# Attention stage of a fused block: softmax sums of two branches added up by POOL, shared product sets, single exact-pass buffers

## The reference, cut to what matters

```python
o1 = _attn(q, k1, v1, causal[None, None])          # causal, 1024 keys
o2 = _attn(q, ks, vs)                              # selected, KEEP = 256 keys
o3 = _attn(q, kw, vw, winmask[None, None])         # window of 64 keys
o = g[:, 0] * o1 + g[:, 1] * o2 + g[:, 2] * o3
return o.transpose(0, 2, 1, 3).reshape(B, T, N_HEAD * VDIM) @ Wproj
```

## Time and profile before

| | |
|---|---|
| median of 3 runs | 2780.97 us (2780.05 to 2782.86) |
| the profiled execution | 2781.34 us |
| its span | 2779.4 us |
| mean granted TensorE clock | 0.908 |
| busy over the span: TensorE, its weight loads | 83%, 56% |
| busy: VectorE, ScalarE, POOL | 59%, 46%, 24% |
| DMA | 360.53 MB, mean 130 GB/s |
| exponentials, L1370 | x1600, 637.8 us in total |
| products with ones, L1344 | x3200, 512.0 us |
| products with causal values, L1344 | x1536, 284.3 us |
| reciprocals, L1425 | x192, 331.9 us |

### The profile page before, as it was taken

One profiled execution on the slowest core, in us unless ns is written; L12 is line 12 of the kernel. 1 busy time (PEld: TensorE's weight loads), 2 busy tenths in 40 slices (PEclk: granted clock), 3 DMA queues, 4 the chain that ended last, 5 costly groups with the idle time before them and its releaser, 6 DMA issues. The chain is left out here.

```text
span 2779.4 us, 45396 instructions
## 1 busy us (share of the span) xinstructions
PE 2320.6 (83%) x16656; PEld 1545.5 (56%) x16656; DVE 1628.3 (59%) x3043; ACT 1266.2 (46%) x2777; POOL 669.8 (24%) x687
## 2 busy tenths in 40 slices
PE   5585858663999999999999999999999999601995
PEld 3464545442666666666666666566566666401884
DVE  4758575734466466466566576566565564450766
ACT  2354545440455555555455455555555555310442
POOL 0265656573011011011011011011010010145332
PEclk9697978765999999999999999999999999655997
DMA  2255555479547646556655565664664660611113
GB/s 97 97 219 184 216 187 201 172 269 226 126 93 146 132 101 139 122 118 131 127 121 122 120 136 114 136 129 104 137 137 96 138 130 10 158 39 47 48 53 110
DMA packets 222841, 360.53 MB, mean 130 GB/s; under 512 B 68794, under 2 KB 124701, under 8 KB 222240
## 3 DMA queue, kind: packets, MB, share of 16 engines
q1 hardware_dynamic: 216288, 348.43, 50.1%
q0 software_dynamic: 4320, 8.43, 0.9%
q10 hardware_dynamic: 2016, 0.77, 0.2%
HBM read 229.58 MB, written 126.56 MB: 128 GB/s over the span
## 5 line engine op out<-in xcount | busy, mean ns | idle before, releaser
L1370 ACT ACTIVATE prob<-ps 128x512 f32<-128x512 f32 (+5 forms) x1600 | 637.8, 441 | 665.8 <-PE ps L1325 656.3
L1434 DVE TENSOR_REDUCE maxima<-ps 128x1 f32<-128x512 f32 (+3 forms) x768 | 387.5, 547 | 291.4 <-PE ps L1250 147.0
L1344 PE MATMUL ps<-prob,plain 128*32 128x512 f32 (+5 forms) x3200 | 512.0, 443 | 0.0
L1400 POOL TENSOR_TENSOR products<-products,sums 128x256 f32<-128x256 f32 x192 | 140.8, 733 | 1540.3 <-DVE sums L1425 1539.0
L1439 DVE TENSOR_REDUCE maxima<-ps 128x2 f32<-128x512 f32 (+1 forms) x512 | 293.7, 606 | 192.6 <-PE ps L1261 98.4
L1425 DVE RECIPROCAL sums<-sums 128x256 f32<-128x256 f32 x192 | 331.9, 1736 | 97.6 <-ACT sums L1383 97.6
L1317 PE MATMUL ps<-q1a_s,k1a_s 128*128 128x512 f32 (+3 forms) x768 | 303.0, 395 | 0.0
L1325 PE MATMUL ps<-q1b_s,k1b_s 128*128 128x512 f32 (+3 forms) x768 | 301.1, 393 | 0.0
L1344 PE MATMUL ps<-prob,v_s 128*32 128x512 f32 (+3 forms) x1536 | 284.3, 491 | 0.0
L1250 PE MATMUL ps<-k1a_s,q1a_s 128*128 128x512 f32 (+3 forms) x768 | 234.5, 374 | 0.5 <-DVE maxima L1439 0.2
L1381 ACT ACTIVATE products<-ps,gates_a 64x512 f32<-64x512 f32 x192 | 131.0, 682 | 196.4 <-PE ps L1344 196.3
(11 more groups left out here) (333 smaller groups left out, 4889.8 us busy)
## 6 DMA issues: line engine op xcount, KB each, us to landing
qh_dram<-pairs SPq DMA_DIRECT2D x96, 512.0 KB, 2.7
kwh_dram<-pairs SPq DMA_DIRECT2D x64, 512.0 KB, 2.7
qa_s<-qh_dram SPq DMA_DIRECT2D x128, 256.0 KB, 4.7
kwa_s<-kwh_dram SPq DMA_DIRECT2D x128, 256.0 KB, 7.7
q1a_s<-qh_dram SPq DMA_DIRECT2D x128, 256.0 KB, 4.8
qb_s<-qh_dram SPq DMA_DIRECT2D x64, 256.0 KB, 9.3
kwb_s<-kwh_dram SPq DMA_DIRECT2D x64, 256.0 KB, 10.3
k1a_s<-k1ah_dram SPq DMA_DIRECT2D x32, 512.0 KB, 6.9
```

The source lines that it names most:

```text
L1344: mm = pe.matmul(ps[at:at + VD, SCORES + k % 2, q0 - c * CH:q0 - c * CH + w], w_, m.prob[:, n % PROBS, h, 0:w], start=first, stop=True, sk ...
L1370: act.activation(m.prob[:, u % PROBS, h, 0:w], ps[:, turn % SCORES, 0:w], ACT.Exp, scale=SCALE).then_inc(s["exp_done"], 1)
L1400: pool.tensor_tensor(o, o, m.sums[:, br, cc], ALU.mult).then_inc(s["divided"], 1)
L1434: ins = dve.tensor_reduce(partial[:, h, i, part:part + 1], bank[:, 0:w], AX, ALU.max)
```

## The change

- SUMS is ordered window, selected, causal, and UNITS is made of groups: the window units in sets of up to two as before, each still with its own ones; then each of the eight units of selected 0, selected 1 and causal 0 is zipped with one of the eight of causal 1, of equal width.
- In a zipped group no ones are multiplied. The first unit's two heads take the lower 64 rows of a bank, the second's the upper 64: `product(side, u, NW * place, values)`.
- The sums of the selected and causal branch are made from `acc`: POOL adds the exponentials of all key tiles of a (branch, half), both heads in one instruction (steps "acc", 12 a side, one with a copy ahead). At the end TensorE multiplies `acc` with ones ("total": four matmuls of 512 columns into one fill bank, once per branch and side), and ScalarE copies that out ("take"). The total of the selected branch comes in the same window after the set of units 15 and 16, that of the causal branch in the next window, behind the scores and the fill of unit 0. "divide" of these branches waits for "take".
- PROBS goes from 4 to 6; a buffer is reused only after POOL's add of it too.
- qb, kwb, ksb, vw and vs have one buffer. They are loaded by local_exact(side), which waits for the products of the first LOCAL units of side - 1. LOCAL is now 16. SyncE's order is whole(side), local_exact(side), rows 2 and 1, local(side + 1) (now qa, kwa, ksa; the same wait as before by its formula, with the new LOCAL), row 0.

```diff
+SUMS = [(2, 0), (2, 1), (1, 0), (1, 1), (0, 0), (0, 1)]
-SUMS = [(1, 0), (2, 0), (1, 1), (2, 1), (0, 0), (0, 1)]
+    sets = [found[2, c][i:i + 2] for c in range(NC) for i in range(0, len(found[2, c]), 2)]
+    short = found[1, 0] + found[1, 1] + found[0, 0]
+    return sets + [list(x) for x in zip(short, found[0, 1])]
+LAST = [max(u for u, x in enumerate(UNITS) if x[:2] == k) for k in SUMS]
 LOCAL = LAST[3] + 1
-PROBS = 4
+PROBS = 6
...
+    if w > 0:
+        pieces = closing(w - 1)
     for u in range(len(UNITS) + 1):
         if u < len(UNITS):
             todo.append(("scores", w, u))
+            todo += [("acc", w, op) for op, x in enumerate(SUMMING) if x[0] == u]
+        ready = [group for group, follower in zip(TOGETHER, TOGETHER[1:] + [(len(UNITS),)]) if follower[0] == u]
+        for group in ready:
+            todo.append(("products", w, group))
+            for done in sorted(LAST.index(x) for x in group if x in LAST):
+                todo.append(("sum", w, done))
+                if SUMS[done][0] == 2 and w % 2 == 1:
+                    pieces += [("divide", w, done, piece) for piece in range(PIECES)]
+                if SUMS[done] == (1, NC - 1):
+                    pieces += total_and_divide(w, 1)
         todo += pieces[:1]
         pieces = pieces[1:]
+    return todo + pieces + (closing(w) if w == SIDES - 1 else [])
...
+def total_and_divide(w, br):
+    pieces = [("total", w, br), ("take", w, br)]
+    for c in range(NC):
+        if w % 2 == 1:
+            pieces += [("divide", w, SUMS.index((br, c)), piece) for piece in range(PIECES)]
+            if br == 0:
+                pieces.append(("proj", w, c))
+    return pieces
...
+            def local_exact(side):
+                if side >= 1:
+                    sp.wait_ge(s["products_done"], len(UNITS) * (side - 1) + LOCAL)
...
             for side in range(1, SIDES):
                 whole(side)
+                local_exact(side)
+                for br in (2, 1):
+                    row(side, br)
                 if side + 1 < SIDES:
                     local(side + 1)
-                for br in (2, 1, 0):
-                    row(side, br)
+                row(side, 0)
...
+                elif kind == "total":
+                    pe.wait_ge(s["acc_done"], len(SUMMING) * side + max(n for n, x in enumerate(SUMMING) if x[1] == a[0]) + 1)
+                    for c in range(NC):
+                        for h in range(HP):
+                            at = c * NW + h * VD
+                            mm = pe.matmul(bank[at:at + VD, :], m.plain[:], m.acc[:, a[0], c, h, :], start=True, stop=True,
+                                           skip_group_check=True)
...
+                    if br == 2:
+                        product(side, u, 0, values)
+                        mm = product(side, u, NW, [m.plain[:]] * HP)
+                    else:
+                        mm = product(side, u, NW * place, values)
+                    mm.then_inc(s["products_done"], 1)
...
+                        if old in RELEASED:
+                            act.wait_ge(s["acc_done"], len(SUMMING) * old_side + RELEASED[old])
...
+                if kind == "take":
+                    act.wait_ge(s["fill_ready"], n + 1)
+                    for c in range(NC):
+                        ins = act.copy(m.sums[rows, br, c * CH:(c + 1) * CH],
+                                       ps[c * NW:(c + 1) * NW, 8 - SPARES + n % SPARES, :])
+                    ins.then_inc(s["taken"], 1)
...
+            for step in plan.of(("divide", "acc")):
+                if step[0] == "acc":
+                    pool.wait_ge(s["exp_done"], HP * (n + u + 1))
+                    if side > 0:
+                        pool.wait_ge(s["fill_ready"], plan.fill_no["total", side - 1, br] + 1)
+                    if former is None:
+                        pool.wait_ge(s["acc_done"], len(SUMMING) * side + op)
+                        ins = pool.tensor_tensor(total, total, new[:, :, 0:w], ALU.add)
+                    else:
+                        if UNITS[former][4] > UNITS[u][4]:
+                            pool.tensor_copy(m.acc[:, br, c, :, 0:alone], old[:, :, 0:alone])
+                        ins = pool.tensor_tensor(total, old[:, :, 0:w], new[:, :, 0:w], ALU.add)
+                    ins.then_inc(s["acc_done"], 1)
...
-                if br == 2:
+                if br == 1:
                     pool.wait_ge(s["divided"], nth)
+                    pool.tensor_tensor(o, o, m.products[:, 2, cc], ALU.add).then_inc(s["o_done"], 1)
```

More of the change, by code:

```diff
@@ L1025, in exact_pass, with closing @@
             todo.append(("scores", w, u))
[L1026 to L1036, removed]
+            todo += [("acc", w, op) for op, x in enumerate(SUMMING) if x[0] == u]
[8 more added lines that the diff above has]
+                    pieces += total_and_divide(w, 1)
         todo += pieces[:1]
         pieces = pieces[1:]
-    return todo + pieces
+    return todo + pieces + (closing(w) if w == SIDES - 1 else [])
[7 more added lines that the diff above has]
+    return pieces
+def closing(w):
+    return total_and_divide(w, 0)
 def window(w, prepare):
@@ L1071, in __init__ @@
         self.steps = steps
-        self.fills = self.of(("max0", "max1", "max2", "rows", "proj"))
+        self.fills = self.of(("max0", "max1", "max2", "rows", "proj", "total"))
         self.fill_no = {x: n for n, x in enumerate(self.fills)}
+        by_dve = [x for x in self.fills if x[0] != "total"]
+        self.emptied = {x: n + 1 for n, x in enumerate(by_dve)}
+        self.taken = {x[1:]: n + 1 for n, x in enumerate(self.of(("take",)))}
         self.divisions = {x: n + 1 for n, x in enumerate(self.of(("divide",)))}
-        self.ends = {x[:2]: n + 1 for n, x in enumerate(self.fills)}
+        self.ends = {x[:2]: n + 1 for n, x in enumerate(by_dve)}
     def of(self, kinds):
@@ L1146, in local @@
                 k, src = side % 2, kept[side // NSIDE]
-                g, own = side % NSIDE // 2, side % NSIDE
+                g = side % NSIDE // 2
                 if side >= 2:
@@ L1243, in fill @@
                 if n >= SPARES:
-                    pe.wait_ge(s["emptied"], n - SPARES + 1)
+                    former = plan.fills[n - SPARES]
+                    if former[0] == "total":
+                        pe.wait_ge(s["taken"], plan.taken[former[1:]])
+                    else:
+                        pe.wait_ge(s["emptied"], plan.emptied[former])
                 bank, k = ps[:, 8 - SPARES + n % SPARES, :], side % 2
@@ L1316, in scores @@
                     bank = ps[:, turn % SCORES, 0:w]
-                    pe.matmul(bank, kx, qx[:, k, h, q0:q0 + w], start=True, stop=False, skip_group_check=True)
+                    pe.matmul(bank, kx, qx[:, h, q0:q0 + w], start=True, stop=False, skip_group_check=True)
                     at = q0 - j * P
@@ new lines, in product @@
+                n, k = side * len(UNITS) + u, SUMS.index((br, c))
+                first = UNITS.index(next(x for x in UNITS if x[:2] == (br, c))) == u
+                if first and side * len(SUMS) + OCCUPANTS[k] > 0:
+                    pe.wait_ge(s["banks_free"], side * len(SUMS) + OCCUPANTS[k])
+                for h in range(HP):
+                    mm = pe.matmul(ps[at + h * VD:at + (h + 1) * VD, bank_of(side, k), q0 - c * CH:q0 - c * CH + w],
+                                   weights[h], m.prob[:, n % PROBS, h, 0:w], start=first, stop=True,
+                                   skip_group_check=True)
@@ L1423, in _ @@
                     total = m.sums[:, br, c * CH + piece * w:c * CH + (piece + 1) * w]
-                    dve.wait_ge(s["banks_free"], side * len(SUMS) + k + 1)
+                    if br == 2:
+                        dve.wait_ge(s["banks_free"], side * len(SUMS) + k + 1)
+                    else:
+                        dve.wait_ge(s["taken"], plan.taken[side, br])
                     dve.reciprocal(total, total).then_inc(s["inverse_done"], 1)
-                if step not in plan.fill_no:
+                if step not in plan.emptied:
                     continue
```

146 lines of the change are left out of this document (91 added, 55 removed).

## The result

The changed kernel takes 3050.27 us (median of 4 runs, 3046.15 to 3059.08) beside 2781.91 us for the kernel before: a ratio of **1.0965** (95% interval 1.0933 to 1.0996), slower by 268 us. Forecast were 2935 us, at most 3020. The direction was right, the size was not.

A forecast was written before the change was run, and what follows sets the result against it. TensorE was taken to bound the attention stage at full clock. A pair of windows, -7.8 + 0.75 + 1.4 + 9.2 + 4.4 + 3 = +11.0 us, gave +154 in all: 2935 us, range 2755 to 3020.

The forecast's parts named there:

- passes removed, edges: TensorE in the attention stage: fewer product passes save 7.8 us a pair of windows, stretch edges cost 0.75.
- waits, net of before's: TensorE's new waits a pair of windows: 1.4 us for exp and bank, 9.2 for loads, 4.4 for causal divisions.
- clock: TensorE's clock falls after the load wait; only odd windows pay, 3 us a pair (bounds 0 and 6).
- The edge left out by the prediction: Selected branch's total behind a product set: taken to have no edge; with one, 12 us more over the kernel.
- The loads: Each window's start: operands land 19.5 us after release against 14.9 of work; TensorE waits 4.6, 9.2 a pair.
- The divisions: Even windows' heads: projections wait 2.1 and 3.2 us for causal divisions, 0.9 before; 4.4 a pair.
- POOL: POOL's sums take 22 us of 52 a window, ending 19.3 after release in odd windows, covered by landing: cost 0.
- rival (a): Loads hidden but POOL not: odd windows wait 4.7 us for the total, +3.4 a pair; 2821 us, chance 0.12.
- the closing chain: At the kernel's end, the last side's total and take add 3 us.
- (b): Faster: TensorE's work covers the loads, nothing new waits; 2684 us, or 2754 with projection waits kept; chance 0.15.
- (c): Worse: clock falls in every window, POOL's last add ends 3 us past the landing; 3025 us, chance 0.12.
- (d): Two units in four tiles do not run side by side: 5.6 us a window return, over 3100; chance 0.02.

The follow-up runs named there:

- e9: Changed kernel with window-only operands loaded earlier, divisions moved beside the even windows' own scores, and both projections one further turn later: 2728.22 us, ratio 0.9818.
- e1: Changed kernel with the window-only operands (kwb, vw, kwa) released after 9 window units, the rest kept: 2889.70 us, ratio 1.0396.
- e7: e1 with eight extra matmuls ahead of the row 0 transposition at an odd window's end and of each projection: 2859.51 us, ratio 1.0279.
- e5: e1 with the selected and causal divisions moved beside the even windows' own scores, projections two turns after their last division: 2754.80 us, ratio 0.9901.
- e8: Changed kernel with the divisions and projections moved as in e5, loads released as the change has them: 2994.19 us, ratio 1.0772.
- e2: Changed kernel with twenty matmuls of 512 columns, their result overwritten, ahead of the first max2 fill of a window: 2995.66 us, ratio 1.0781.

## Why the prediction was right in direction and wrong in size

e9 does the same TensorE work as the changed kernel at clock 1.00 throughout, so it tells apart what the timeline of the changed kernel mixes. A pair of windows, forecast and measured:

| term | forecast | measured | from |
|---|---|---|---|
| passes removed, edges | -7.05 | -4.9 | busy of e9, 98.5, less before, 103.3 |
| waits, net of before's | +15.0 | +14.7 | length less busy: 17.0 after, 2.3 before |
| clock | +3 | +7.4 | busy of after, 105.9, less e9, 98.5 |
| sum | +11.0 | +17.3 | |

In the 15 pairs that is 94 us more than forecast: 66 of them clock, 32 from the passes and edges, less 4 for the waits. The rest of the 112 us between 2935 and the profiled 3047 us lies in the last window (14) and the start (4).

**The step that failed is the clock**: "The head of an even window waits for divisions anyway; odd ones pay: 3 a pair". Odd windows did pay 2.8 (50.1 busy against 47.3 in e9). The even ones paid 4.6 (55.8 against 51.2), more than the odd. The reasoning had it the wrong way round: the waits for divisions gave no cover to slow matmuls, they brought the clock down themselves. At the openings and in the heads of the 15 even windows it fell 34 times: 15 at the 2.10 us for row 0, which the prediction does not have, 4 at the first projection and 15 at the second. The waits at the projections were forecast, with their sizes, and then only counted by their length. e1 and e7 show the rest: waits of at most 2.3 us were enough, with no load late, and filling them brought the clock back. With the rule that the prediction takes from the Trainium skill (TensorE: Matmul & The Clock Gate, HAM oscillation — how this bites in real kernels), by which every window would pay, 6 a pair, the trace agrees in that every window paid, 7.4 a pair; but in the even ones the clock fell at waits for VectorE and not for a DMA. The row of an 8.79 us wait was no reason to halve it: the clock stood at 0.50 before that wait began, with TensorE busy, as this stretch of the kernel before shows.

```profile
680.00:690.00 10.00, 8.53 (x26) 5.05 (x25) 8.80 (x18) 0.00 (x0) 0.00 (x0) 0.50 1.06 216
```

**Passes removed**, forecast -7.8 and 0.75 for edges. By the starts in TensorE's timeline the products with ones, the products with causal and selected values and the totals fell by 110 us in 30 windows between before and e9, 7.3 a pair: near. But scores, masks, row transpositions and fills, unchanged in number, took 41 us more, 2.7 a pair against 0.75 (counted by starts; by busy time the net is 0.3 better). What lengthens them was not tested. The edge left out by the prediction, that of the selected total behind a product set, is not the cause: in e9 that total starts 0.42 us after the set's last start, where starts within the set are 0.44 apart, so the rule on tiling modes that the prediction takes from the Trainium skill (TensorEngine Tiling, Key Properties) agrees with the trace there.

```profile
1489.12 0.62 PE L1449 MATMUL ps<-prob,vs_s 128*32 128x512 f32 x2
1489.14 0.62 PE L1449 MATMUL ps<-prob,v_s 128*32 128x512 f32 x2
1489.58 0.60 PE L1449 MATMUL ps<-prob,vs_s 128*32 128x512 f32 x2
1489.59 0.60 PE L1449 MATMUL ps<-prob,v_s 128*32 128x512 f32 x2
1490.01 1.04 PE L1394 MATMUL ps<-acc,plain 128*32 128x512 f32 x8
```

**The loads.** Landing forecast 19.5 us after the release: SyncE's first issue at 1593.10 to the first max2 at 1613.05 is 19.95, and 19.7 in the next window. The wait came to 133.7 us in 30 windows, 8.9 a pair against 9.2. It is not the same in both windows, as forecast (4.6 each), but 6.0 and 2.9 in the mean, because the 2.10 us for row 0 at the odd window's end stand inside the landing time.

**The divisions.** Waits at the projections rose from 1.2 to 3.6 a pair, +2.4 against +4.4. What the prediction missed is the odd window's end: the transposition of row 0 waits 2.10 us for its maxima. The selected divisions there put VectorE behind; with them moved (e5, e8) that wait is gone. Together 4.5, so that term was right by luck.

**POOL.** Adds of 256, 512, 768 and 1024 elements took 0.724, 1.272, 1.828 and 2.377 us, against estimates of 0.73, 1.27, 1.80 and 2.34. Hidden in the changed kernel, as forecast. In e1 its wait showed at 1.2 us a pair, not the 4.7 of rival (a). The 2.10 us for row 0 and the slow work behind them stand ahead of it there; with TensorE kept busy through them (e7) it is 2.39.

**The last window** has no loads to wait for, and there POOL's queue shows in the open. TensorE's timeline of e9, whose closing part is that of the change:

```profile
2298.15 1.06 PE L1394 MATMUL ps<-acc,plain 128*32 128x512 f32 x8 [1.91 <-POOL acc L1553]
2317.67 1.93 PE L1394 MATMUL ps<-acc,plain 128*32 128x512 f32 x8 [8.62 <-POOL acc L1546]
```

From the opening of window 31 to the end the execution takes 458.8 us after and 445.9 before: +13, where +3 for the closing chain and -3.5 for the window were forecast. The changed kernel's trace has the same two waits, of 1.89 and 8.61 us, once each. At the start the change gained 6 us of the forecast 10.5. Neither was taken apart further.

**The rivals.** (b), faster, needed the loads and the divisions covered; in the changed kernel neither is, and with both out of the way (e9) the gain is 51 us. The 97 forecast for it would have needed no idle and no lengthened scores. (c) had the clock falling in every window, which is right, but ascribed the rest to POOL, for which TensorE did not wait in any of these windows; 3025, still 25 short. (d) is wrong: in the rows above the matmuls of two units start 0.01 us apart, and the next ones 0.44 later.

## What to carry to other kernels

Once TensorE bounds a kernel at full clock, price a new wait by its length and by the slow work behind it, short waits and those for other engines too: here 14.7 us of waits in a pair cost 22.1. When tiles are shared and units reordered, check which unit each buffer's release now stands behind, buffer by buffer, not for the group; the buffers read only by early units can go early. Two hidden delays side by side have to be mended together: each alone gave back 160 and 56 us, both 295, and only then was the change worth making.

## What had not been expected of the hardware

- TensorE's granted clock fell to 0.50 at a wait of 2.30 us for VectorE in 15 of 15 even windows (e1), and 600 or 360 useless matmuls put into waits made a kernel faster, by 55 us (e2) and 30 us (e7).
- The eight matmuls of a total took 1.04 us at full clock and 1.94 behind a wait. Their mean length in the trace was 820 ns after and 605 ns in e9, and that of the exact pass's 128x192 scores from qa and kwa 377 and 314 ns, so the mean length of one shape shows the clock. Not of every shape: the scores of 64 columns took 270 and 272 ns.
- POOL was busy for 840 of the 1528 us of e9's 30 windows (before: 11 of 100), and a reciprocal on VectorE took 1736 ns beside it, 1737 before.
